# Routed experts of the second layer in shared blocks: column tiles of 64 and 32 slots on TensorE

## The chip, the cores and the metric

The kernel runs on one core of one Trainium2 chip. The metric is the device time of one execution in microseconds (us), taken as the median of several runs. A profiled execution gives the trace from which all rows below are read.

## What is computed

A transformer of two layers over 4 x 256 = 1024 tokens of width 256. Each layer is `x + attention(layernorm(x))` and then `x + ffn(layernorm(x))`. The change lies in the feed-forward part of the second layer, a mixture of 60 routed experts of which each token takes four, beside a shared expert:

```python
logits = x @ gate_w.T
probs = jax.nn.softmax(logits.astype(jnp.float32), axis=-1)
weights, sel = jax.lax.top_k(probs, TOP_K)            # TOP_K = 4 of E = 60
cw = jnp.zeros((M, E), jnp.float32).at[jnp.arange(M)[:, None], sel].add(weights)
def step(acc, ews):
    w13_e, w2_e, cw_e = ews                           # w13: 2 * 176 x 256, w2: 256 x 176
    gu_e = x @ w13_e.T
    h = jax.nn.silu(gu_e[:, :I]) * gu_e[:, I:]
    return (acc + cw_e[:, None] * (h @ w2_e.T), None)
sparse, _ = jax.lax.scan(step, jnp.zeros((M, H), jnp.float32), (w13, w2, cw.T))
return (shared + sparse).reshape(orig_shape)
```

1024 tokens with four experts each are 4096 pairs, on average 68 per expert. The counts per expert follow from the reference's routing of its inputs.

## The kernel before

Five instruction streams run side by side: PE (matmuls), ACT, DVE, POOL (which also issues the indirect DMAs) and SP (which issues the weight loads). They meet at semaphores. All matmuls of this part are float32; each of them shows as two records in the trace.

The second layer's feed-forward is two parts of one block of instructions.

`route_shared_l1` computes the router and the shared expert. DVE turns the routing into a table: a token's rank within its expert gives a slot of a block of 128 slots, block e for expert e, and slots past 128 of an expert go to further blocks behind the 60, which are handed out in expert order. Two tables result, `m.row` (the row of each slot) and `m.row_w` (its weight). They are built by matmuls of one-hot matrices (`table`, line 1846; DVE fills at lines 2003 and 2006, one tile of tokens after the other) that are interleaved by hand with the matmuls of the shared expert (lines 1812 and 1828). `further_blocks` (lines 1713 to 1723) then works out how many further blocks there are and which expert each serves; it ends with `over_ready`. POOL fetches the first eight blocks' rows in this part.

`routed_l1` works through the blocks. For block b:

- POOL gathers 128 rows of x from DRAM (`fetch`, line 1728), eight blocks ahead of the scatter (`FETCH`).
- PE turns them (`turn_x`, line 2099, two transposes, three blocks ahead); ACT copies (line 2161).
- PE multiplies with `w13` (`gate_up`, line 2111, two matmuls of 352 streamed columns, two blocks ahead). The stationary operand is the block's tokens (128 columns); the expert's weights stream.
- ACT takes the SiLU (line 2167), DVE multiplies (line 2193), PE turns the hidden rows (`turn_hid`, line 2120, one block ahead), ACT copies (line 2180).
- PE multiplies with `w2` (`outputs`, line 2132, two matmuls of 256 columns, 88 rows each).
- DVE scales by `row_w` into one of four buffers (line 2207), POOL scatters 128 rows to DRAM (`send`, line 2072).

So PE's order within a step is turn_x(b + 3), gate_up(b + 2), turn_hid(b + 1), outputs(b). Weights of 24 experts lie in SBUF as a ring (`RING`), loaded in pairs; twelve experts are loaded before the feed-forward part and twelve during it. SP reloads a pair's place when `outputs` of both its blocks has run (`y_ps`). For a further block SP reads the expert's number from memory (`load_further`, lines 1702 to 1710).

`all_rounds` sets the order: every engine waits for `over_ready` and loads the count of further blocks (line 2039) before its first block; it then runs 60 blocks, and behind nested tests of the count (line 2044) up to three rounds of twelve. Each round drains the order above and starts it anew. When all scatters have landed, `combine_and_store` reads each token's four rows, adds them and stores the result.

## Time and profile before

| | us |
|---|---|
| median of 3 runs | 832.78 (830.38 to 833.06) |
| span of the profiled execution, first to last instruction | 796.0 |
| median less span | 36.8 |
| routed stage, first gate_up matmul to last matmul | 582.5 to 764.7 |
| last scatter issued by POOL | 772.8 |
| combine and store | 776.9 to 796.0 |

| engine | busy us of the span |
|---|---|
| PE matmul | 677.6 (85%) |
| DVE | 439.8 (55%) |
| ACT | 322.9 (41%) |
| POOL | 298.2 (37%) |

A time for the profiled execution itself, other than its span, is not listed, so the 36.8 us stand for what lies around the span. The trace has 72 scatters: 60 blocks and one round of twelve. Matmul records overlap: a record is longer than the distance to the next start. Busy shares of PE are therefore read together with the distance between starts.

### The profile page before, as it was taken

How to read it: one execution, taken by the hardware profiler on the slowest of the kernel's cores; microseconds unless marked ns; L12 is line 12 of the kernel's file. 1: busy time of each engine (PE TensorE's matmuls, PEld its weight loads, DVE VectorE, ACT ScalarE, POOL GpSimd, SP SyncE). 2: the span in 40 equal slices, each digit the busy share in tenths (PEclk: the TensorE clock that was granted, in tenths of full speed). 3: DMA queues.
4: the chain of work that ended last, by engine and by line, in shares of the span. 5: the costliest groups of instructions: out<-in, count | busy, mean ns of one | idle time of the engine just before them, and what ended most of it. 6: DMA issues, size and time to landing. Idle time of an engine off the chain costs nothing. (4 is left out here: it accounts for less than half of the span.)

```text
span 796.0 us, 12037 instructions
## 1 busy us (share of the span) xinstructions
PE 677.6 (85%) x3794; PEld 441.6 (55%) x3794; DVE 439.8 (55%) x1182; ACT 322.9 (41%) x666; POOL 298.2 (37%) x449
## 2 busy tenths in 40 slices
PE   1667888895999999995699995999999999999940
PEld 1443444453766666763455563657677677777730
DVE  4658888854404569677776634589513333333315
ACT  1324777873232223421366673321243333333310
POOL 5440111101234233222013332122567777777760
PEclk9976999997699999997789997799999999999985
DMA  3185222001402555447343101950149999996347
GB/s 112 35 267 156 62 62 63 22 2 44 125 1 66 150 175 175 146 146 186 76 121 82 44 2 32 313 160 0 30 107 307 268 286 290 295 304 230 100 104 264
DMA packets 82904, 107.62 MB, mean 135 GB/s; under 512 B 10707, under 2 KB 57004, under 8 KB 82836
## 3 DMA queue, kind: packets, MB, share of 16 engines
q1 hardware_dynamic: 72820, 83.07, 35.3%
q0 software_dynamic: 7808, 20.05, 9.3%
q10 hardware_dynamic: 2208, 3.67, 1.2%
q8 instruction: 34, 0.56, 0.3%
q14 instruction: 34, 0.28, 0.1%
HBM read 82.47 MB, written 24.14 MB: 134 GB/s over the span
## 5 line engine op out<-in xcount | busy, mean ns | idle before, releaser
L769 DVE TENSOR_REDUCE l_mx<-ps 128x2 f32<-128x512 f32 (+2 forms) x256 | 125.7, 550 | 43.9 <-PE ps L629 43.6
L857 ACT ACTIVATE l_prob<-ps 128x1024 f32<-128x1024 f32 x96 | 98.5, 1027 | 25.5 <-PE ps L659 25.2
L629 PE MATMUL ps<-l_ks,l_qs 48*128 48x256 bf16 (+1 forms) x384 | 71.7, 300 | 26.0 <-DMA l_qs<-l_q_stacks 12.9
L1728 POOL DMA_INDIRECT xg<-x_rows,r_empty x80 | 78.9, 987 | 28.8 <-issue 19.8
L1392 DVE SCALAR_TENSOR_TENSOR xs<-ps,comb,xs 128x256 f32<-128x256 f32 x128 | 55.8, 481 | 59.3 <-PE ps L1052 59.2
L2072 POOL DMA_INDIRECT y_rows<-r_at_blk,row x72 | 71.5, 993 | 24.1 <-issue 17.4
L2193 DVE TENSOR_TENSOR r_hot<-r_hot,ps 128x176 f32<-128x176 f32 x72 | 24.3, 338 | 91.6 <-ACT r_hot L2167 91.6
L674 PE MATMUL ps<-l_prob,v 128*9 128x256 f32 (+1 forms) x768 | 69.9, 388 | 1.1 <-ACT l_prob L857 1.1
L1141 POOL TENSOR_TENSOR r_ehid<-r_erelu 128x512 f32<-128x512 f32 x32 | 35.6, 1112 | 83.5 <-ACT r_erelu L1245 83.5
L629 PEld LDWEIGHTS ps<-l_ks,l_qs 48*128 48x128 bf16 (+1 forms) x384 | 29.6, 102 | 57.6 <-issue 21.3
L1052 PE MATMUL ps<-f_w,r_ehid 128*128 128x256 f32 x256 | 60.8, 380 | 0.2
L2207 DVE TENSOR_SCALAR r_at_blk<-ps,row_w 128x256 f32<-128x256 f32 x72 | 34.8, 484 | 46.1 <-DMA y_rows<-r_at_blk,row 25.8
L1052 PEld LDWEIGHTS ps<-f_w,r_ehid 128*128 128x128 f32 x256 | 48.4, 190 | 21.1 <-issue 13.9
L1041 PE MATMUL ps<-xT,f_w 128*128 128x512 f32 x128 | 60.0, 592 | 0.0
L597 POOL TENSOR_TENSOR attn<-rest,l_rec 128x32 f32<-128x32 f32 x64 | 14.5, 247 | 113.7 <-DVE l_rec L788 113.7
L659 PE MATMUL ps<-l_qs,l_ks 50*128 50x256 bf16 (+1 forms) x384 | 56.5, 281 | 0.0
L2161 ACT COPY r_at_low<-ps 128x256 f32<-128x256 f32 x75 | 27.8, 372 | 55.6 <-PE ps L2099 55.6
L597 POOL TENSOR_TENSOR l_ctxv<-rest,l_rec 128x64 f32<-128x64 f32 x64 | 17.7, 298 | 82.7 <-DVE l_rec L788 82.7
L2111 PE MATMUL ps<-ew,r_at_low 128*128 128x352 f32 x144 | 48.5, 460 | 0.0
L2111 PE MATMUL ps<-ew13b,r_at_low 128*128 128x352 f32 x144 | 48.4, 459 | 0.0
L2167 ACT ACTIVATE r_hot<-ps 128x176 f32<-128x176 f32 x72 | 22.9, 318 | 59.0 <-PE ps L2111 59.0
L1812 PE MATMUL ps<-xT,r_sw 128*128 128x512 f32 x88 | 41.7, 614 | 0.0
(278 smaller groups left out, 1224.0 us busy)
## 6 DMA issues: line engine op xcount, KB each, us to landing
ew<-in_L_w SPq DMA_DIRECT2D x18, 704.0 KB
ew13b<-in_L_w SPq DMA_DIRECT2D x12, 704.0 KB
f_w<-in_L_w SPq DMA_DIRECT2D x32, 256.0 KB, 2.9
ew<-in_L_w SPq DMA_DIRECT2D x18, 352.0 KB
ew2b<-in_L_w SPq DMA_DIRECT2D x12, 352.0 KB
ew13b<-in_L_w SPq DMA_DIRECT2D x12, 352.0 KB
l_k_stacks<-part SPq DMA_DIRECT2D x8, 384.0 KB, 3.5
l_ks<-l_k_stacks SPq DMA_DIRECT2D x32, 96.0 KB, 2.3
```

The costliest lines, as they stand in the source:

```text
L629: ins = nc.tensor.matmul(ps[:, score_bank(n) + k, qt * S:(qt + 1) * S], qs[row:row + R, u % NBUF, col, qt * P:(qt + 1) * P], ks[row:row + ...
L659: ins = nc.tensor.matmul(ps[:, 2 + 2 * (n % 2) + k, kt * S:(kt + 1) * S], ks[row:row + lay.krows, b, col, kt * P:(kt + 1) * P], qs[row:row ...
L674: ins = nc.tensor.matmul(ps[row:row + W, 6, (c % 2) * S:(c % 2 + 1) * S], v[:, n // UP // GR * QT + kt, head, :], prob[:, n % PROBS, k, kt ...
L769: ins = nc.vector.reduce_max(mx[:, u % 2, :, s, head], one[:, :, lo:hi], AX_X)
L857: nc.scalar.activation(prob[:, n % PROBS, :, :, :].rearrange("p h k q -> p (h k q)"), ps[:, 2 + 2 * (n % 2):4 + 2 * (n % 2), :].rearrange( ...
L1041: ins = nc.tensor.matmul(m.ps[:, n % 2, :], m.f0_up[:, n % WSLOTS, c, :], m.xT[:, c, half * HT:(half + 1) * HT], start=(c == 0), stop=(c = ...
L1052: nc.tensor.matmul(m.ps[:, 2 + t, 0:D], ehid[:, n % 2, t * P:(t + 1) * P], m.f0_down[:, n % WSLOTS, :], start=True, stop=True).then_inc(e_ ...
L1392: v.scalar_tensor_tensor(m.xs[:, i, :], m.ps[:, 2 + t, 0:D], m.comb[:, i, e:e + 1], m.xs[:, i, :], ALU.mult, ALU.add).then_inc(e_added, 1)
L1728: nc.gpsimd.indirect_dma_start(m.xg[:, b % XBUF, :], None, m.x_rows, bass.IndirectOffsetOnAxis(m.token[:, b:b + 1], 0)).then_inc(m.x_loade ...
L1812: ins = nc.tensor.matmul(ps[:, 2 * (q % 2) + a, :], sw13[:, k, own], m.xT[:, k, h * TILES * P:(h + 1) * TILES * P], start=(k == 0), stop=( ...
L2072: nc.gpsimd.indirect_dma_start(m.y_rows, bass.IndirectOffsetOnAxis(m.row[:, b:b + 1], 0), yb[:, b % YBUF, :], None).then_inc(y_sent[b % YB ...
L2111: ins = nc.tensor.matmul(ps[:, b % 2, 0:2 * I1], xgT[:, b % 4, c * P:(c + 1) * P], w13[:, s, c, :], start=(c == 0), stop=(c == KD - 1))
```

## The change

Four experts share three blocks. Of each expert the first 64 tokens take half of block 3g or 3g + 1 of its group g; the next 32 take a quarter of block 3g + 2. Tokens past 96 go to units of 64 slots, two to a block, behind the 45 shared blocks. Which columns of a block belong to which expert is fixed in `tenants`; gate_up and outputs issue one matmul per tenant and half of the contraction, with the tenant's 64 or 32 tokens as the stationary operand and the tenant's weights streaming, into that tenant's partitions of PSUM. Eight unit blocks always run (`FIRST` = 45 + 8); the count is tested for more than 16, 32 and 48 units. The order of a step is kept, and it now runs through the rounds without draining: each engine runs to `FIRST - ahead`, then waits for `over_ready`, loads the count and tests it, and either goes on into the next round or runs its last `ahead` steps (SP 8, POOL 8, PE 3, ACT 3, DVE 2). PE's first transposes wait for `table_read` instead. A pair's place in the ring is reloaded after the third block of its group. POOL no longer fetches beyond the last block.

The routing on DVE changes with it: the counts are compared with 15 marks instead of 7, the slot of a token takes three cases instead of two, and tables have 77 columns instead of 96. One more small load, `starts`, brings the group offsets.

```diff
-ROUND = 12
-OVER = -(-(T * TOP1 // P) // ROUND) * ROUND
-BLOCKS = E1 + OVER
-FURTHER = OVER // ROUND
+HALF, FULL = 64, 96
+BASE = E1 // 4 * 3
+ROUND, FURTHER = 8, 3
+FIRST = BASE + ROUND
+BLOCKS = FIRST + FURTHER * ROUND
+OVER = 2 * (BLOCKS - BASE)
+MARKS = -(-(T - FULL) // HALF)
+SPARE = -(-BLOCKS // TOP1)
...
+def tenants(b):
+
+    if b >= BASE:
+        w = E1 + 2 * (b - BASE)
+        return ((0, HALF, w), (HALF, HALF, w + 1))
+    g, r = divmod(b, 3)
+    if r < 2:
+        return ((0, HALF, 4 * g + 2 * r), (HALF, HALF, 4 * g + 2 * r + 1))
+    return tuple((k * (FULL - HALF), FULL - HALF, 4 * g + k) for k in range(4))
+
+
+def pair_first(b):
+
+    return None if b < BASE and b % 3 == 2 else tenants(b)[0][2] // 2
+
+
+def pair_last(q):
+
+    return 3 * (q // 2) + 2 if 2 * q < E1 else BASE + q - E1 // 2
+
+
+def slot_starts():
+
+    e = np.arange(E1)
+    whole = 3 * P * (e // 4) + HALF * (e % 4)
+    rest = 3 * P * (e // 4) + 2 * P + (FULL - HALF) * (e % 4) - HALF - whole
+    return np.stack([whole, rest, BASE * P - FULL - whole - rest]).astype(np.float32)
...
-def further_blocks(nc, link, m, cmp, over_f, incl):
-
-    v, iota, half = nc.vector, m.iota, OVER // 2
-    for a in range(2):
-        own = slice(a * half, (a + 1) * half)
-        link(v.tensor_tensor(cmp, bcast(incl[:], 1, half), bcast(iota[:, own], 2, E1), ALU.is_le))
-        link(v.tensor_reduce(over_f[:, 1 + a * half:1 + (a + 1) * half], cmp, AX_X, ALU.add))
+def further_blocks(nc, link, m, flat, over_f, incl):
+
+    v, iota, own = nc.vector, m.iota, 2 * ROUND
+    cmp = flat[:, 0:own * E1].rearrange("p (o e) -> p o e", e=E1)
+    for a in range(0, OVER, own):
+        link(v.tensor_tensor(cmp, bcast(incl[:], 1, own), bcast(iota[:, a:a + own], 2, E1), ALU.is_le))
+        link(v.tensor_reduce(over_f[:, 1 + a:1 + a + own], cmp, AX_X, ALU.add))
     v.tensor_copy(over_f[:, 0:1], incl[:, E1 - 1:E1])
-    link(v.tensor_scalar(cmp[:, 0, 0:OVER], over_f[:, 1:1 + OVER], float(E1 - 1), None, ALU.min))
+    link(v.tensor_scalar(flat[:, 0:OVER], over_f[:, 1:1 + OVER], float(E1 - 1), None, ALU.min))
     v.tensor_copy(m.over[:, 0:1], over_f[0:1, 0:1])
-    v.tensor_copy(m.over[:, 1:1 + OVER], cmp[0:1, 0, 0:OVER]).then_inc(m.over_ready, 1)
+    v.tensor_copy(m.over[:, 1:1 + OVER], flat[0:1, 0:OVER]).then_inc(m.over_ready, 1)
...
+        sp.dma_start(starts[:], io["starts"].partition_broadcast(P)).then_inc(ld, 16)
...
-        link(v.tensor_tensor(many, bcast(count[:], 2, NT - 1), bcast(marks[:, 0:NT - 1], 1, E1), ALU.is_gt))
+        link(v.tensor_tensor(many, bcast(count[:], 2, MARKS), bcast(marks[:], 1, E1), ALU.is_gt))
...
-        link(v.tensor_tensor(extra[:], count[:], iota[:, 0:E1], ALU.subtract))
-        link(v.tensor_scalar(shift[:], extra[:], float(E1 - 1), float(P), ALU.add, ALU.mult))
+        link(v.scalar_tensor_tensor(shift[:], count[:], float(HALF), starts[:, 2, :], ALU.mult, ALU.add))
         rank = ps[:, 7, 0:NT * E1].rearrange("p (i e) -> p i e", i=NT)
-        link(v.tensor_scalar(prob[:], rank, float(P), None, ALU.is_ge))
-        link(v.tensor_tensor(slot_of, prob[:], bcast(shift[:], 1, NT), ALU.mult))
-        link(v.tensor_tensor(prob[:], slot_of, rank, ALU.add))
-        link(v.scalar_tensor_tensor(slot_of, bcast(iota[:, 0:E1], 1, NT), float(P), prob[:], ALU.mult, ALU.add))
+        v.scalar_tensor_tensor(prob[:], rank, float(HALF), bcast(starts[:, 1, :], 1, NT), ALU.is_ge, ALU.mult)
+        link(v.scalar_tensor_tensor(slot_of, rank, float(FULL), bcast(shift[:], 1, NT), ALU.is_ge, ALU.mult))
+        link(v.tensor_tensor(prob[:], prob[:], slot_of, ALU.add))
+        link(v.tensor_tensor(slot_of, rank, bcast(starts[:, 0, :], 1, NT), ALU.add))
+        link(v.tensor_tensor(slot_of, slot_of, prob[:], ALU.add))
...
-        v.tensor_copy(m.row_w[:], ps[:, 6, BLOCKS:2 * BLOCKS])
-        further_blocks(nc, link, m, over_cmp, over_f, incl)
+        v.tensor_copy(m.row_w[:], ps[:, 6, BLOCKS:2 * BLOCKS]).then_inc(m.table_read, 1)
+        further_blocks(nc, link, m, blk_flat, over_f, incl)
...
-    def all_rounds(eng, run, settled=lambda last: None):
-
+    def all_rounds(eng, ahead, step):
+
+        for b in range(FIRST - ahead):
+            step(b, FIRST)
         eng.wait_ge(m.over_ready, 1)
-        blocks = eng.value_load(m.over[0:1, 0:1], min_val=0, max_val=OVER)
-        run(0, E1)
+        units = eng.value_load(m.over[0:1, 0:1], min_val=0, max_val=OVER)
         def further(r):
-            if r < FURTHER:
-                with eng.If(blocks > r * ROUND):
-                    run(E1 + r * ROUND, E1 + (r + 1) * ROUND)
-                    further(r + 1)
-                    settled(E1 + (r + 1) * ROUND)
+            end = FIRST + r * ROUND
+            if r == FURTHER:
+                for b in range(end - ahead, end):
+                    step(b, end)
+                return
+            with eng.If(units > 2 * (r + 1) * ROUND):
+                for b in range(end - ahead, end + ROUND - ahead):
+                    step(b, end + ROUND)
+                further(r + 1)
+            with eng.Else():
+                for b in range(end - ahead, end):
+                    step(b, end)
         further(0)
-        settled(E1)
     @block.sync
     def _(sp):
-        def loads(first, last):
-            for b in range(max(first, RING), last, 2):
-                sp.wait_ge(y_ps, b - RING + 2)
-                if b < E1:
-                    load_weights(sp, m, io, b)
+        def load(b, end):
+            q = pair_first(b)
+            if q is not None and q >= RING // 2:
+                sp.wait_ge(y_ps, pair_last(q - RING // 2) + 1)
+                if 2 * q < E1:
+                    load_weights(sp, m, io, 2 * q)
                 else:
-                    load_further(sp, m, io, b)
-        all_rounds(sp, loads)
+                    load_further(sp, m, io, 2 * q)
+        all_rounds(sp, ROUND, load)
...
-        def run(first, last):
-            for b in range(first, last):
-                if b + FETCH < BLOCKS:
-                    fetch(b + FETCH)
-                send(b)
-
-        def settled(last):
-            for b in range(last, min(last + FETCH, BLOCKS)):
-                pool.wait_ge(x_loaded[b % XBUF], 16 * (b // XBUF + 1))
-            for b in range(last - YBUF, last):
-                pool.wait_ge(y_sent[b % YBUF], 16 * (b // YBUF + 1))
+        def step(b, end):
+            if b + FETCH < end:
+                fetch(b + FETCH)
+            send(b)
+            if b == end - 1:
+                for a in range(end - YBUF, end):
+                    pool.wait_ge(y_sent[a % YBUF], 16 * (a // YBUF + 1))
         pool.wait_ge(m.added, NT)
-        all_rounds(pool, run, settled)
+        all_rounds(pool, FETCH, step)
...
-            w13, _, s = ring_slot(m, b)
-            if b % 2 == 0:
-                pe.wait_ge(m.ew_loaded[b % RING // 2], ring_loads(b))
+            q = pair_first(b)
+            if q is not None:
+                pe.wait_ge(m.ew_loaded[q % (RING // 2)], ring_loads(q))
             pe.wait_ge(xt_done, b + 1)
             if b >= 2:
                 pe.wait_ge(hid_done, b - 1)
             for c in range(KD):
-                ins = nc.tensor.matmul(ps[:, b % 2, 0:2 * I1], xgT[:, b % 4, c * P:(c + 1) * P], w13[:, s, c, :],
-                                       start=(c == 0), stop=(c == KD - 1))
+                for row, n, w in tenants(b):
+                    w13, _, s = ring_slot(m, w)
+                    ins = nc.tensor.matmul(ps[row:row + n, b % 2, 0:2 * I1], xgT[:, b % 4, c * P + row:c * P + row + n],
+                                           w13[:, s, c, :], start=(c == 0), stop=(c == KD - 1))
             ins.then_inc(gu_ps, 1)
...
-            _, w2, s = ring_slot(m, b)
             pe.wait_ge(ht_done, b + 1)
             if b == 0:
                 pe.wait_ge(m.y_copied, NT)
             if b >= 2:
                 pe.wait_ge(y_done, b - 1)
             for c in range(2):
-                ins = nc.tensor.matmul(ps[:, 4 + b % 2, 0:D], hidT[:, b % 2, c * P:(c + 1) * P], w2[:, s, c, :],
-                                       start=(c == 0), stop=(c == 1))
+                for row, n, w in tenants(b):
+                    _, w2, s = ring_slot(m, w)
+                    ins = nc.tensor.matmul(ps[row:row + n, 4 + b % 2, 0:D], hidT[:, b % 2, c * P + row:c * P + row + n],
+                                           w2[:, s, c, :], start=(c == 0), stop=(c == 1))
             ins.then_inc(y_ps, 1)
-        def run(first, last):
-            if first == 0:
-                for b in range(3):
-                    turn_x(b)
-                m.last_outputs()
-                pe.wait_ge(m.shared_read, UNITS)
-            gate_up(first)
-            gate_up(first + 1)
-            turn_hid(first)
-            for b in range(first, last):
-                if b + 3 < BLOCKS:
-                    turn_x(b + 3)
-                if b + 2 < last:
-                    gate_up(b + 2)
-                if b + 1 < last:
-                    turn_hid(b + 1)
-                outputs(b)
-        all_rounds(pe, run)
+        def step(b, end):
+            if b + 3 < end:
+                turn_x(b + 3)
+            if b + 2 < end:
+                gate_up(b + 2)
+            if b + 1 < end:
+                turn_hid(b + 1)
+            outputs(b)
+
+        pe.wait_ge(m.table_read, 1)
+        for b in range(3):
+            turn_x(b)
+        m.last_outputs()
+        pe.wait_ge(m.shared_read, UNITS)
+        gate_up(0)
+        gate_up(1)
+        turn_hid(0)
+        all_rounds(pe, 3, step)
```

ACT and DVE are given the same form as PE: their work per block is as before, as `step(b, end)`, with 3 and 2 steps ahead. The number of blocks, 96 in the buffers before, is 77.

## Rows read from the trace of the kernel before

**Rows 1.** The first line of the page

```profile
span 796.0 us, 12037 instructions
```

**Rows 2.** Windows: us; busy PE, PEld, DVE, ACT, POOL; clock, DMA share, GB/s

```profile
680.00:720.00 40.00, 40.00 (x194) 29.59 (x193) 12.92 (x32) 15.53 (x49) 30.47 (x31) 1.00 0.99 302
```

**Rows 3.** Timeline, PE, one block: start, us, engine, line, shapes, count

```profile
659.87 1.35 PE L2111 MATMUL ps<-ew,r_at_low 128*128 128x352 f32 x4
...
661.05 0.38 PE L2120 MATMUL ps<-ident,r_hot 128*88 128x128 f32 x2
...
661.27 1.03 PE L2132 MATMUL ps<-ew,r_hot 88*128 88x256 f32 x4
...
662.36 1.35 PE L2111 MATMUL ps<-ew,r_at_low 128*128 128x352 f32 x4
```

**Rows 4.** The chain of waits, its end; start, us, what

```profile
756.07 0.97 POOL xg L1728
...
757.35 0.99 POOL y_rows L2072
...
772.79 3.17 DMA y_rows<-r_at_blk,row
...
776.88 4.64 DMA ew13b<-y_rows
```

**Rows 5.** Timeline, first and last matmuls of the stage, one scaling

```profile
582.46 2.63 PE L2111 MATMUL ps<-ew,r_at_low 128*128 128x352 f32 x8
...
762.06 0.48 DVE L2207 TENSOR_SCALAR r_at_blk<-ps,row_w 128x256 f32<-128x256 f32 x1 [0.40 <-PE ps L2132]
...
763.64 1.03 PE L2132 MATMUL ps<-ew2b,r_hot 88*128 88x256 f32 x4
```

**Rows 6.** Timeline, PE, attention of the first layer

```profile
100.31 0.39 PE L629 MATMUL ps<-l_ks,l_qs 48*128 48x256 bf16 x2
...
100.63 1.05 PE L674 MATMUL ps<-l_prob,v 128*9 128x256 f32 x16
...
101.61 0.44 PE L687 MATMUL ps<-ident,l_sumsT 128*128 128x128 f32 x2
```

**Rows 7.** Timeline, PE, attention of the second layer

```profile
431.22 1.06 PE L674 MATMUL ps<-l_prob,v 128*34 128x256 f32 x8
```

**Rows 8.** Windows, attention of the second layer

```profile
440.00:478.00 38.00, 36.48 (x275) 22.01 (x276) 19.38 (x65) 27.94 (x52) 12.84 (x46) 1.00 0.09 24
```

**Rows 9.** DMA over 591 to 733 by queue; one SP timeline row

```profile
DMA packets 16411, 40.40 MB, mean 284 GB/s; under 512 B 2546, under 2 KB 2546, under 8 KB 16396
...
q1 hardware_dynamic: 11178, 25.96, 59.8%
...
q0 software_dynamic: 5218, 14.27, 35.9%
...
590.32 25.73 SPq L1698 DMA_DIRECT2D ew<-in_L_w  x12
```

**Rows 10.** Lines 2044, 2039: instructions, ns min/median/max, first to last start

```profile
L2044 PEldq COMPARE_BRANCH  x2: 93/2386/4680, 733.3 to 763.5; - x2
...
L2044 ACTq COMPARE_BRANCH  x2: 44/47/50, 733.7 to 763.8; - x2
...
L2044 DVEq COMPARE_BRANCH  x2: 55/59/63, 734.6 to 766.8; - x2
...
L2039 PEldq TENSOR_LOAD <-over x1: 486/486/486, 575.1 to 575.1; - x1
...
L2039 PEldq FUSED_REGOPS  x1: 170/170/170, 575.6 to 575.6; - x1
```

**Rows 11.** DVE: two groups by line (busy, mean ns), one timeline row

```profile
L1979 DVE TENSOR_TENSOR r_at_blk<-r_count,r_marks 128x420 f32<-128x420 f32 x1 | 0.6, 596 | 0.0
...
L1718 DVE TENSOR_TENSOR r_at_blk<-r_incl,iota 128x1080 f32<-128x1080 f32 x2 | 2.6, 1278 | 0.0
...
584.30 0.34 DVE L2193 TENSOR_TENSOR r_hot<-r_hot,ps 128x176 f32<-128x176 f32 x1 [13.73 <-ACT r_hot L2167]
```

More of the change, by code:

```diff
@@ L1955, in _ @@
         v.memset(ones_e[:], 1.0)
-        v.tensor_scalar(marks[:], iota[:, 1:1 + NT], float(P), None, ALU.mult)
+        v.tensor_scalar(marks[:], iota[:, 0:MARKS], float(HALF), float(FULL), ALU.mult, ALU.add)
         dve.wait_ge(logit_ps, 1)
@@ L2363, in host_layout @@
     io["empty"] = np.arange(ROWS, ROWS + BLOCKS, dtype=np.float32)
+    io["starts"] = slot_starts()
     io["upper"] = np.triu(np.ones((P, P), np.float32), 1)
```

78 lines of the change are left out of this document (38 added, 40 removed).

## Prediction

> **What bounds the kernel now.** I read the windows by stage first. In the routed stage of the second layer PE is busy without a break at full granted clock, and the DMA engines are at 0.99 as well [rows 2]; so two resources are near their limit, and neither busy share names the bound. The timeline of one block gives PE's period: its gate_up matmuls start at 659.87 and those of the next block at 662.36, so 2.49 us, with no gap between any two groups [rows 3]. The chain of waits then shows that the end is not PE's: from 755 on (and from 725, rows alike) it runs through POOL alone, a gather and a scatter per block, 756.07 to 758.65, so 0.97 + 0.30 + 0.99 + 0.30 = 2.57 us with issue [rows 4]. PE's last matmuls run until 764.67 (763.64 + 1.03) [rows 5], while POOL sends its last rows at 772.79; their landing (3.17), 0.92 of settling and the combine from 776.88 close the span of 796.0 [rows 1, 4]. So the stage goes at POOL's pace, 2.57 per block, with PE 0.08 behind and DMA behind that.
>
> The time outside the span is 832.8 - 796.0 = 36.8 us; I have no other time for the profiled execution, so the sum is made on the span and the median added.
>
> **How many blocks.** The reference's routing of its inputs gives experts of 3 to 181 tokens. Eight exceed 128, hence one round of 12 further blocks: 72, as the trace has it (72 scalings and scatters). Past 96 there are exactly 16 units of 64 (14 experts are over 96; those of 178 and 181 take two, the other twelve, from 97 to 151, one). 16 fits the first 8 unit blocks, so 45 + 8 = 53 blocks run, and the test for more than 16 fails. No count lies on a threshold (the nearest below 97 is 88; below 160, 151), so rounding will not add a seventeenth.
>
> **Removed: 19 blocks.** POOL now does 45 times 2.57 plus 8 scatters alone at 1.29 (no fetch past the last block), 126 us, if never kept waiting. POOL stops being the bound; next late is PE, below.
>
> **Added: column tiles on PE.** Each gate_up and output matmul becomes two of 64 or four of 32 columns, each with its own weights streaming. If tiles of one set stream together, a set takes as long as one full matmul. The first layer's value matmuls have that form, f32 with 256 streamed columns in four column tiles: 16 records take 1.05 us [rows 6], where 4 full-width records of 256 columns take 1.03 [rows 3]. So four go at once. In the second layer, with two tiles of 34 columns, 8 records take 1.06 [rows 7]: two at once. I take the stream time of a block as unchanged.
>
> What is not free is the change between full and tiled array, four times per block (turn_x full, gate_up tiled, turn_hid full, outputs tiled). In full mode a group starts 0.17 or 0.16 before the recorded end of the one ahead (661.22 and 661.05; 661.43 and 661.27) [rows 3], since the records overlap. Into the tiles it is 0.07 (100.70 and 100.63), out of them 0.07 (101.68 and 101.61) [rows 6]: a gap of 0.10 each way. The first step in tiles is longer, by 0.03 with 34 columns (1.06 against 1.03); for 64 I take 0.05, bounds 0 and 0.10. The first transpose behind tiles is 0.06 longer (two take 0.44, in full mode 0.38); for the narrower turn_hid less, so 0.05. Per block: 4 x 0.10 + 2 x 0.05 + 2 x 0.05 = 0.60, so 3.09 us; bounds 2.9 and 3.2.
>
> The Trainium skill (TensorE: Matmul & The Clock Gate, Part 3, "The mechanism") says that a weight load overlaps a running matmul only when its row group differs, which column tiles of one block never do. The trace speaks against it: 16 records in the time of 4 leave no room for loads between them. By that rule the time would be that of the third rival.
>
> PE: 72 blocks took 764.67 - 582.46 = 182.2 us [rows 5], 2.9 over 72 x 2.49. Now 2.9 + 53 x 3.09 = 166.7, end 749.2.
>
> **The tail.** POOL no longer lags, so the scatter follows PE: 0.04 to DVE, 0.48 scaling [rows 5], 0.3 to POOL, 3.17 landing, 0.92 settling = 4.9: combine from 754.1 instead of 776.9, its 19.1 us unchanged. Span 773.2.
>
> **Moved: the count's test.** Loading the unit count and the If stood before the loop and between rounds; now every engine meets both shortly before its last steps. On PE: the load and the operation behind it 0.49 + 0.17, then the branch. Untaken it cost 0.09, taken 4.68, when PE had no work left after 764.67 [rows 5, 10]. Now the failed test jumps with three blocks still to finish. I take 0.7 + 4.68 less the 1.2 of matmuls under which the old branch began: +4.2, bounds 0 and 4.9. ACT's and DVE's branches show 0.05 and 0.06 [rows 10], but nothing that they do right after, so their price is 0 to 4.7 too: ACT's would lie beside PE's; DVE's comes after scaling block 50 with only 2.3 us of PE work left, so up to +3.7; I take 0, the row. SP's and POOL's meet slack (POOL needs 1.29 per block there against PE's 3.09, and has four y buffers).
>
> The Trainium skill (Runtime: NRT & Kernel Launch, "Instruction fetch mechanics") has a taken branch outside the fetched window wait for a fetch. If that holds for DVE as for PE, the upper bound of this term applies.
>
> **DMA.** Weights: 25.96 MB for 48 experts, 0.541 each [rows 9]; now 36 + 16 = 52, 28.1 MB, and 98 gathers and scatters of 0.131 MB, 12.8. At the 284 GB/s of 591 to 733 that is 144 us from about 593 (the first ring load was at 590.3 [rows 9] and now waits a block more, since three blocks free four experts): last weights at 737, 5.3 us of PE work behind them, 742.5. PE needs until 749: hidden by 7 us. Slower than 262 GB/s it would set the end.
>
> **Small edits.** The count comparison grows from 420 to 900 elements, twice (0.60 for 420, 1.28 for 1080: +0.5 each), one more 480-element operation (+0.7), one of 60 fewer (-0.2): DVE's first table is 1.5 us later and PE waits for it. Against that 64 table fills and 64 table matmuls shrink from 96 and 192 to 77 and 154 columns: 1.3 us on DVE (0.02 per fill, by the 1.0 ns per element of those two rows), 2.0 on PE (38 columns of 0.83 ns), spread over the stage. Net 0, bounds -2 and +1.5. further_blocks: 8 operations of 960 (1.15 each) for 4 of 1.28, +4 us in DVE's 13.7 idle [rows 11]; PE waits for the row weights now, not for it. One 0.7 KB load, at stage start: 0. SP's unit loads keep their form.
>
> Sum: 773.2 + 4.2 = 777.4 span, **814.2 us**, -2.2%.
>
> **Rivals.**
> - DMA floor: gaps cheaper, branch hidden; the end is 742.5 + 4.9 + 19.1 = 766.5, time 803; with 300 GB/s 801. For: the windows show 302 [rows 2]. Against: gaps seen in both attentions. 0.17.
> - Costlier finish: DVE's jump exposed, or DMA near 260 GB/s: 818 to 824. For: 4.68 on PE. 0.19.
> - Weight loads exposed in every step: eight steps per block at the 0.06 above, two counted already, +0.36 x 53 = 19: 829 to 833, no change. Against: [rows 6, 7]. 0.06. (The skill's rule on row groups, above, would act so.)
> - Slower: tiles stream one after the other. A 64-column block then costs one more 2.05 us of streaming (2.49 less four transposes of 0.11), a 32-column one three more: 38 x 2.05 + 15 x 6.15 = 170 us, time 984. It decides from a loss of 0.35 us per block (18.6 / 53), a sixth of the streaming. Against: [rows 6, 7]; for: those have 9 and 34 columns and the same 128 rows, outputs here use 88. 0.06.
> - Clock: gaps drop the grant to 1.2 GHz. The attention with the same gaps ran at 1.00, PE busy 36.5 of 38 [rows 8]; at half clock far slower, above 900. 0.03. A seventeenth unit, eight more blocks, +24: 838. 0.01.
>
> **How the numbers follow.** Forecast (809 to 817) 0.48. Range 801 to 825 holds 0.84: forecast, floor, costlier finish. A measurement tells about 0.3%, 2.5 us. Faster: 0.84 and half of the fourth case, 0.87; within 0.03; slower 0.10.
>
> **What would show it.** 544 gate_up records (38 x 8 + 15 x 16) in 53 blocks; block starts 3.0 to 3.2 apart with gaps of 0.10 at each change; POOL waiting for DVE; last PE work near 753, the combine from about 758; one branch on PE over 4 us shortly before its end. Wrong if the blocks' period is over 3.4, if PE waits for weights, or if the clock is below 1.00 in the loop.

## The result, and the profile after

| | before | after |
|---|---|---|
| median, us | 832.92 (830.38 to 835.52) | 779.86 (777.43 to 781.93) |
| ratio after/before | | 0.938, 95% interval 0.9348 to 0.9413 |
| span of the profiled execution | 796.0 | 776.8 |
| that execution's own time | not listed | 778.58 |

The change takes 53 us, not the 18.6 of the forecast, and the time lies below the whole range. Yet the forecast of the span was 777.4, and the span is 776.8. Both can be so only because the 36.8 us that I put outside the span do not lie there. One execution of the kernel before took 876.85 us at a granted clock of 0.80, and it is in no comparison below.

The changed kernel: the page's first line; the timeline of PE over two blocks (start, us, engine, line, shapes, count); the failed test and the last matmuls; the end of the chain of waits.

```profile
span 776.8 us, 12603 instructions
```

```profile
640.83 1.40 PE L2152 MATMUL ps<-ew,r_at_low 128*64 128x352 f32 x8
642.16 0.42 PE L2161 MATMUL ps<-ident,r_hot 128*88 128x128 f32 x2
642.51 1.07 PE L2174 MATMUL ps<-ew2b,r_hot 88*32 88x256 f32 x16
643.51 0.44 PE L2138 MATMUL ps<-ident,xg 128*128 128x128 f32 x2
643.88 1.39 PE L2152 MATMUL ps<-ew,r_at_low 128*32 128x352 f32 x16
645.20 0.42 PE L2161 MATMUL ps<-ident,r_hot 128*88 128x128 f32 x2
645.55 1.08 PE L2174 MATMUL ps<-ew,r_hot 88*64 88x256 f32 x8
646.57 0.44 PE L2138 MATMUL ps<-ident,xg 128*128 128x128 f32 x2
646.94 1.40 PE L2152 MATMUL ps<-ew,r_at_low 128*64 128x352 f32 x8
```

```profile
748.38 1.40 PE L2152 MATMUL ps<-ew,r_at_low 128*64 128x352 f32 x8 [2.02 <-issue]
...
751.42 1.95 PE L2174 MATMUL ps<-ew,r_hot 88*64 88x256 f32 x16
```

```profile
754.82 2.49 DMA y_rows<-r_at_blk,row
757.73 4.63 DMA ew13b<-y_rows
```

In this kernel gate_up is L2152, turn_hid L2161, outputs L2174, turn_x L2138. Eight records (two tiles of 64 columns) take 1.40 us and sixteen (four tiles of 32) take 1.39, where four at full width take 1.35 [rows 3]: the tiles of a set stream together. Blocks start at 640.83, 643.88 and 646.94, a period of 3.06. A group now starts 0.06 or 0.07 before the recorded end of the one ahead, where in full mode it is 0.16 or 0.17: the gap of 0.10 at each change that the attentions showed [rows 6]. The Trainium skill (TensorEngine Tiling (Array Packing), "Key Properties") says that a change of tiling mode drains TensorE; the trace agrees in so far as each change shows this gap.

### The profile page after: what moved, and what is told of

The parts are those of the page before. It is cut to its first block and busy times, and to the rows that moved or that the text cites. A ratio compares the mean times of both kernels' runs of the same rounds, so it can differ in the third digit from the quotient of the medians.

```text
span 776.8 us, 12603 instructions
## 1 busy us (share of the span) xinstructions
PE 658.9 (85%) x4224; PEld 377.0 (49%) x4224; DVE 427.4 (55%) x1148; ACT 304.9 (39%) x606; POOL 253.7 (33%) x403
## 5 line engine op out<-in xcount | busy, mean ns | idle before, releaser
L2115 POOL DMA_INDIRECT y_rows<-r_at_blk,row x53 | 52.3, 987 | 59.4 <-DVE r_at_blk L2245 51.9
L2234 DVE TENSOR_TENSOR r_hot<-r_hot,ps 128x176 f32<-128x176 f32 x53 | 17.9, 338 | 82.5 <-ACT r_hot L2209 43.9
L1761 POOL DMA_INDIRECT xg<-x_rows,r_empty x53 | 53.1, 1002 | 18.8 <-issue 14.5
L2245 DVE TENSOR_SCALAR r_at_blk<-ps,row_w 128x256 f32<-128x256 f32 x53 | 25.6, 483 | 51.5 <-remote 24.8
L2203 ACT COPY r_at_low<-ps 128x256 f32<-128x256 f32 x53 | 19.7, 373 | 59.4 <-PE ps L2138 33.9
L2152 PE MATMUL ps<-ew,r_at_low 128*64 128x352 f32 (+1 forms) x304 | 40.9, 468 | 2.3 <-issue 2.3
L674 PEld LDWEIGHTS ps<-l_prob,v 128*9 128x9 f32 (+1 forms) x768 | 26.8, 98 | 23.0 <-issue 10.2
L2209 ACT ACTIVATE r_hot<-ps 128x176 f32<-128x176 f32 x53 | 16.9, 320 | 51.9 <-PE ps L2152 25.5
```

The costliest lines, as they stand in the source:

```text
L674: ins = nc.tensor.matmul(ps[row:row + W, 6, (c % 2) * S:(c % 2 + 1) * S], v[:, n // UP // GR * QT + kt, head, :], prob[:, n % PROBS, k, kt ...
L1761: nc.gpsimd.indirect_dma_start(m.xg[:, b % XBUF, :], None, m.x_rows, bass.IndirectOffsetOnAxis(m.token[:, b:b + 1], 0)).then_inc(m.x_loade ...
L2115: nc.gpsimd.indirect_dma_start(m.y_rows, bass.IndirectOffsetOnAxis(m.row[:, b:b + 1], 0), yb[:, b % YBUF, :], None).then_inc(y_sent[b % YB ...
L2152: ins = nc.tensor.matmul(ps[row:row + n, b % 2, 0:2 * I1], xgT[:, b % 4, c * P + row:c * P + row + n], w13[:, s, c, :], start=(c == 0), st ...
```

## Experiments

Ratios are to the kernel before on the same chip, with 95% intervals. "Late starts" are a count of my own over a trace: for each of four hand-overs, the k-th group on PE against the k-th instruction that reads it on ACT or DVE, as L2099 to the copy L2161; late is a start over 0.3 us after both the recorded end of the group and the end of what ran before on the reader's engine. The recorded end of a matmul is the profile's model, but semaphore updates have times of their own in the trace.

### The kernel before, once more, and the changed one

> The kernel before, unchanged. Its profiled execution had a span of 796.0 us while its median is 832.9, and the changed kernel's executions take 1.8 us more than their spans (778.58 and 776.8). Theory A: the 36.8 us that I put outside the span lie inside it in the typical execution, so this run's span is near 831 and its trace shows where they go. Rival B: the time around the span really is 35 us for this kernel and 1.8 us for the changed one; then the span is near 796 and the time near 832.

Measured: 833.09 (827.09 to 835.86), ratio 0.9989 [0.9972, 1.0005]. The profiled execution took 827.09 with a span of 825.3: 1.8 us around the span, not 36.8, and 1.7 to 1.9 in every other execution, of all kernels here (776.8 and 778.58 of the changed one). So this profile is one of an ordinary execution, and the one that I read ahead of the prediction, 796.0, is not: with 1.8 it took 797.8, where the 75 others of the kernel before took 826.6 to 839. Where do the 29 us between the two lie? Windows of the ordinary one (us; busy PE, PEld, DVE, ACT, POOL; clock, DMA share, GB/s):

```profile
600.00:640.00 40.00, 35.01 (x161) 24.53 (x160) 10.02 (x25) 12.12 (x39) 26.39 (x27) 0.99 0.92 269
640.00:680.00 40.00, 38.30 (x166) 27.18 (x165) 10.90 (x27) 12.59 (x40) 25.85 (x28) 0.92 0.91 270
680.00:720.00 40.00, 33.09 (x147) 22.32 (x145) 10.03 (x25) 11.69 (x37) 25.37 (x26) 1.00 0.84 253
720.00:760.00 40.00, 34.68 (x155) 24.90 (x156) 10.50 (x26) 12.80 (x40) 25.54 (x26) 0.94 0.55 163
760.00:800.00 40.00, 35.63 (x154) 25.46 (x154) 11.23 (x27) 12.37 (x39) 26.01 (x27) 0.93 0.35 87
```

PE, 40.00 of 40 in the window of [rows 2], is idle for 2 to 7 of 40 us here, and the stage lasts from 580.27 to 796.37, 3.00 per block, in place of 182.2 us and 2.53 [rows 5]. DMA share and traffic fall towards the end; PE doesn't get faster. Over the stage PE is idle for 20.6 us, where the first profile has 1.7. Part of its work is also slower: the granted clock is at half (1.2 GHz) in four stretches of 17.1 us together, each behind idle times of PE, and never in the first profile's stage. Work of 17.1 us at half clock is worth half of that at full clock, so I estimate 9 of the 34 us between the two stages for the clock; the rest is idle time and what PE loses around it. What PE waits for shows in one block of the same trace, PE first, then ACT and DVE:

```profile
592.92 0.38 PE L2099 MATMUL ps<-ident,xg 128*128 128x128 f32 x2
593.14 1.35 PE L2111 MATMUL ps<-ew,r_at_low 128*128 128x352 f32 x4
...
597.19 0.42 PE L2120 MATMUL ps<-ident,r_hot 128*88 128x128 f32 x2 [0.21 <-DVE r_hot L2193]
```

```profile
595.01 0.37 ACT L2161 COPY r_at_low<-ps 128x256 f32<-128x256 f32 x1 [2.39 <-remote]
596.45 0.32 ACT L2167 ACTIVATE r_hot<-ps 128x176 f32<-128x176 f32 x1 [1.06 <-remote]
```

```profile
596.80 0.34 DVE L2193 TENSOR_TENSOR r_hot<-r_hot,ps 128x176 f32<-128x176 f32 x1 [2.71 <-issue]
```

turn_x ended at 593.30, its copy starts at 595.01. gate_up ended at 594.49, its SiLU starts at 596.45, though ACT was free from 595.38. In the trace of before, the same copy and SiLU start 0.04 us behind PE. The update of PE's semaphore has a time in the trace too: 594.99 for this turn_x and 596.42 for this gate_up, 0.02 or 0.03 us before the reader starts. In all 95 late starts of this trace the update stands less than 0.06 us before the start. So the reader is not slow: the signal of a finished matmul comes up to some microseconds late (PE's next groups, at 594.33 and 594.55, have long started by then), and the profile, which looks for a releaser close to the update, often writes "remote" or "issue". From 593 on this holds for 95 of 291 hand-overs behind PE, and never for ACT to DVE (SiLU to product). Before the stage the profile has next to no such wait (two of DVE and none of ACT before 560 in either profile of before, at most).

> The changed kernel, unchanged. Both theories: 778 to 782 us, span 1.8 us less. By theory A its ratio to the kernel before is 0.938 on this chip too.

Measured: 781.46 (780.06 to 785.4), ratio 0.9368 [0.9337, 0.9398]. The saving repeats. Both traces of the changed kernel have late starts too, so its profile was an ordinary one:

| late starts (us in sum) | gate_up to SiLU | turn_x to copy | outputs to scaling | turn_hid to copy |
|---|---|---|---|---|
| before, first profile (72 blocks) | 0 | 0 | 19 (17) | 0 |
| before, second profile (72) | 20 (21) | 28 (42) | 27 (45) | 20 (18) |
| after (53 blocks) | 10 (21) | 17 (22) | 21 (27) | 6 (5) |
| b_noring (72) | 25 (21) | 35 (55) | 33 (50) | 11 (9) |
| b_nogather (72) | 0 | 0 | 0 | 0 |
| b_spgather (72) | 0 | 0 | 0 | 0 |
| b_plainscatter (72) | 1 | 4 | 2 | 1 |
| b_poolbusy (72) | 0 | 2 (4) | 0 | 0 |
| b_twogathers (72) | 17 (23) | 32 (55) | 26 (46) | 12 (11) |
| b_padded (72) | 2 (2) | 2 (4) | 3 (6) | 1 |
| a_nogather (53) | 13 (5) | 0 | 0 | 1 (1) |
| a_full (53) | 14 (15) | 19 (28) | 17 (27) | 9 (11) |
| a_swap (53) | 13 (21) | 28 (25) | 24 (24) | 1 (1) |

The 19 of the first profile are of another kind. PE's signal is there on time in all of them, and the scaling waits until an earlier scatter out of its buffer has landed:

```profile
635.58 0.48 DVE L2207 TENSOR_SCALAR r_at_blk<-ps,row_w 128x256 f32<-128x256 f32 x1 [3.32 <-DMA y_rows<-r_at_blk,row]
```

What makes the signals late was tried with six edits of the kernel before.

### Weights

```diff
-            for b in range(max(first, RING), last, 2):
-                sp.wait_ge(y_ps, b - RING + 2)
-                ...
+            pass
...
```

> The kernel before, leaving out every weight reload of the ring (blocks from the 25th on compute with old weights). In the typical execution of the kernel before, ACT and DVE start 0.5 to 3 us after the PE matmuls that they wait for, in about a quarter of the handoffs; in the trace that the prediction was made from they never do. Theory L-DMA: these late handoffs come with the weight traffic. Then they are gone, POOL's 2.57 us per block is the bound, and the time is 796 to 800. Theory L-POOL: they come with POOL's indirect DMAs, which stay. Then 825 to 833.

Measured: 832.22 (829.06 to 833.04), ratio 0.9976 [0.9948, 1.0004], with as many late starts while the DMA engines ran at 0.27 to 0.29 of their time in place of 0.84 to 0.92. So the weight traffic is not the cause.

### Gathers

```diff
-                if b + FETCH < BLOCKS:
-                    fetch(b + FETCH)
                 send(b)
...
```

> The kernel before, leaving out the gathers of blocks 8 and later (PE turns the first eight blocks' rows again and again; the scaling multiplies by zero so that the scatters stay). Weight reloads and scatters stay. Theory L-POOL: half of POOL's work is gone, late handoffs become fewer or vanish, PE's 2.49 us per block is the bound, time 790 to 797. Theory L-DMA: weight traffic still makes them late, time 812 to 828.

Measured: 788.69 (787.7 to 790.03), ratio 0.945 [0.9425, 0.9476]. Without the gathers on POOL not one start is late, and 44 us are gone: POOL's pace explains 72 x 0.08 = 6 of them at most.

```diff
+        def plain(b):
+            ...
+            sp.dma_start(xg[:, b % XBUF, :], m.x_rows[r:r + P, :]).then_inc(x_plain[b % XBUF], 16)
...
```

> The kernel before with the 64 gathers of blocks 8 to 71 replaced by plain loads of 128 consecutive rows on SyncE's queue, the same bytes read into the same buffers (other rows, and the scaled rows multiplied by zero, so the output is wrong); GpSimd keeps the scatters. L-POOL: what makes TensorE's signals late is GpSimd's descriptor work for the gathers, so few late handoffs, a span like that without gathers: 787 to 793. L-TRAFFIC: it is the read traffic of the rows, so the late handoffs stay, 20 to 30 of 72 at each kind: 815 to 832.

Measured: 798.5 (796.61 to 805.66), ratio 0.9607 [0.9552, 0.9663]. The same bytes are read, the DMA engines are fuller than before, and no start is late:

```profile
600.00:640.00 40.00, 39.09 (x188) 28.28 (x187) 12.17 (x32) 14.75 (x47) 14.76 (x16) 1.00 1.01 296
640.00:680.00 40.00, 38.23 (x181) 27.00 (x180) 11.10 (x30) 14.21 (x45) 14.34 (x15) 1.00 1.01 296
```

PE's idle time here is waiting for its rows (5.7 us of turn_x before DMA xg<-x_rows in 600 to 740), which share a queue with the weights; that is the larger part of the 10 us over b_nogather. So the traffic of the rows alone does not make the signals late; the gathers have to be POOL's.

### Scatters

```diff
-            pool.wait_ge(y_done, b + 1)
-            nc.gpsimd.indirect_dma_start(m.y_rows, bass.IndirectOffsetOnAxis(m.row[:, b:b + 1], 0),
-                                         yb[:, b % YBUF, :], None).then_inc(y_sent[b % YBUF], 16)
+            pass
...
+            act.dma_start(m.y_rows[r:r + P, :], yb[:, b % YBUF, :]).then_inc(y_sent[b % YBUF], 16)
...
```

> The kernel before with its 72 scatters replaced by plain writes of 128 consecutive rows, issued from ScalarE's queue (rows land elsewhere, output wrong); GpSimd keeps the gathers alone, so it is busy half of the time. If gathers alone do it: the late handoffs stay at 20 to 35 of 72 and TensorE, no longer waiting for GpSimd, is still 0.3 to 0.5 us per block over its 2.49: 800 to 825. If it takes gathers and scatters together (GpSimd busy without a pause): few late handoffs, 785 to 795 plus what the 72 issues cost ScalarE.

Measured: 794.02 (792.84 to 795.07), ratio 0.9524 [0.9499, 0.955]. Eight late starts in all. The gathers alone do not do it either. Two fillings of the gap then tell a busy POOL from a POOL busy with indirect DMAs; both keep the scatters' release (`y_done`):

```diff
+            nc.gpsimd.indirect_dma_start(m.spare[:, b % 4, :], None, m.x_rows,
+                                         bass.IndirectOffsetOnAxis(m.token[:, b:b + 1], 0)
+                                         ).then_inc(m.spare_sent[b % 4], 16)
...
```

> The kernel before with each scatter replaced by a second gather of the same block into a spare buffer, released by the same signal (the scaled rows go out as plain writes on ScalarE's queue, other rows, output wrong): GpSimd issues indirect DMAs as before without a pause, but all of one kind. If it is GpSimd's issuing without a pause that makes TensorE's signals late: late handoffs at 20 or more of 72, 815 to 840. If it takes the scatters themselves (writes from SBUF to DRAM by the software queue beside gathers): few of them, 795 to 805.

```diff
+            nc.gpsimd.tensor_tensor(m.spare, m.spare, m.spare, ALU.add).then_inc(spare_set, 1)
...
```

> The kernel before with each scatter replaced by an addition of 128x512 on GpSimd (1.1 us, released by the same signal; the rows go out as plain writes on ScalarE's queue, output wrong): GpSimd as busy as before, with half of the indirect DMAs. If GpSimd's being busy is enough: late handoffs stay, 810 to 835. If it takes indirect DMAs one after the other: few, about the 794 of the kernel without the addition.

Measured: two gathers per block 831.99 (830.35 to 834.4), ratio 1.0028 [1.0009, 1.0048]; a gather and an addition 792.4 (791.56 to 794.87), ratio 0.9564 [0.9527, 0.96]. One window of each, two gathers first:

```profile
640.00:680.00 40.00, 35.91 (x161) 25.20 (x161) 10.02 (x25) 11.83 (x38) 25.89 (x28) 0.96 1.01 309
```

```profile
640.00:680.00 40.00, 40.00 (x194) 29.68 (x193) 13.13 (x32) 15.32 (x48) 32.26 (x33) 1.00 1.02 310
```

With the addition POOL is busier (32.26 of 40 us), the traffic is the same (310 GB/s), and PE has no gap. With a second gather in its place, PE loses 4.1 us of 40. So a busy POOL is not enough, and a gather does as well as a scatter: in these executions it takes two indirect DMAs a block from POOL, one after the other. The pair lies 39.6 us apart, of which 6 at most are POOL's pace (2.57 per block for PE's 2.49).

Two limits of this. First, every edit that takes an indirect DMA away takes its work away from POOL and from the software queue at once; no run tells POOL's issuing from that queue's work. Second, such issuing does not always do it: in the first profile POOL issued 107 indirect DMAs in a row, at most 0.31 us apart (636.34 to 773.78), and no signal of PE was late.

### Why it costs the changed kernel so little

```diff
-            for c in range(KD):
+            for c in (0, 1, 0, 1, 0, 0, 1):
                 ins = nc.tensor.transpose(ps[:, 6 + b % 2, c * P:(c + 1) * P], xg[:, b % XBUF, c * P:(c + 1) * P],
```

> The kernel before with five more transposes in each turn_x (the two of a block repeated into the same places: same result), 0.11 us each, so that TensorE's period without late starts is 2.49 + 0.55 = 3.04 us, about that of the changed kernel, for all 72 blocks. L-SLACK (GpSimd, which needs 2.57 of the period, then has time to catch up, and each hand-over behind TensorE has 0.55 us more before it is missed, so the late starts cost next to nothing): 72 x 3.04 = 219 us after 580, TensorE's end at 800, time 826 to 838, though 40 us of work are added. L-ADD (late starts cost their 0.5 us per block in any case): 860 to 875.

> The same without the gathers of block 8 and on (rows multiplied by zero, output wrong), its control: TensorE's period alone, 822 to 830 by both theories.

Measured: 835.58 (835.09 to 837.12), ratio 1.0069 [1.0047, 1.0092]; its control 829.71 (828.26 to 833.56), ratio 0.9988 [0.9964, 1.0011]. Five more transposes in each of 72 blocks, 40 us of work, cost the kernel before 5 us. PE with them (b_padded), then POOL:

```profile
700.55 1.03 PE L2132 MATMUL ps<-ew2b,r_hot 88*128 88x256 f32 x4
701.42 0.93 PE L2099 MATMUL ps<-ident,xg 128*128 128x128 f32 x7
702.19 1.35 PE L2111 MATMUL ps<-ew13b,r_at_low 128*128 128x352 f32 x4
703.37 0.38 PE L2120 MATMUL ps<-ident,r_hot 128*88 128x128 f32 x2
703.59 1.03 PE L2132 MATMUL ps<-ew2b,r_hot 88*128 88x256 f32 x4
```

```profile
702.39 0.99 POOL L2072 DMA_INDIRECT y_rows<-r_at_blk,row  x1 [0.77 <-DVE r_at_blk L2207]
703.68 0.97 POOL L1728 DMA_INDIRECT xg<-x_rows,r_empty  x1 [0.30 <-issue]
705.42 0.99 POOL L2072 DMA_INDIRECT y_rows<-r_at_blk,row  x1 [0.77 <-DVE r_at_blk L2207]
```

The period is 3.04, POOL waits 0.77 in each block, and only 8 starts are late in the whole trace. I had expected the late starts to stay and their cost to vanish in the slack; they mostly vanish themselves, once POOL pauses in every block. The eight fall between 758 and 773, where the further round begins and POOL issues up to eight indirect DMAs in a row; seven of them come at the fifth of a row or later.

In the changed kernel POOL's slack is as large, but it does not lie in every block. Of the trace of the changed kernel:

```profile
665.63 0.99 POOL L2115 DMA_INDIRECT y_rows<-r_at_blk,row  x1 [2.05 <-DVE r_at_blk L2245]
666.92 0.97 POOL L1761 DMA_INDIRECT xg<-x_rows,r_empty  x1 [0.30 <-issue]
668.19 0.99 POOL L2115 DMA_INDIRECT y_rows<-r_at_blk,row  x1 [0.30 <-issue]
...
675.14 0.99 POOL L2115 DMA_INDIRECT y_rows<-r_at_blk,row  x1 [2.11 <-DVE r_at_blk L2245]
```

A late signal makes POOL wait about 2 us; then it catches up with up to six DMAs in a row, and new late signals fall into that row. By the place of PE's end in POOL's row, 17 of 88 hand-overs are late at the first or second DMA, 25 of 55 at the third or fourth, 12 of 20 at the fifth or sixth, and none of 49 while POOL pauses. In b_padded it is 0 of 196 at the first or second. So rows of DMAs go with late signals within one trace as well; why the first and second differ between the two kernels stays open.

```diff
-            if b + FETCH < end:
-                fetch(b + FETCH)
             send(b)
...
```

> The changed kernel with only the first eight blocks' gathers (later blocks turn the same eight buffers again) and the scaled rows multiplied by zero; the scatters, the weights and every matmul stay, the output is wrong. Theory L-POOL (the late starts behind TensorE come with GpSimd's gathers, and cost the changed kernel little because its period of 3.06 us has slack that the old one had not): no late handoffs, TensorE's last outputs end at 749 to 752 us, time 773 to 778, that is 2 to 7 us under the changed kernel. Rival: the late starts cost per block what they cost before (35 us over 72 blocks, so 26 over 53): 755 to 760, or the weights' floor of 768 if that comes first.

Measured: 772.46 (768.64 to 775.27), ratio 0.9255 [0.921, 0.93] against 0.938 [0.9348, 0.9413] of the changed kernel: 7 us by the medians, 10 by the ratios. The 13 starts over 0.3 us that remain behind gate_up, all in blocks of four tiles, are 0.4 us each and cost nothing, since PE is busy for 40.00 of 40 us in each window between 600 and 720. That is about what the late starts still cost after the change, 0.14 to 0.2 us per block; the trace of the changed kernel has 6.5 us, in ten block periods over 3.06. Before they cost 0.5 per block (832.9 less 797.8, over 72).

### Mode changes, and what lies behind them

```diff
 def tenants(b):
+    return ((0, P, tenants_of(b)[0][2]),)
+
+def tenants_of(b):
...
```

> The changed kernel with one full-width matmul per block and half of the contraction in place of the column tiles (each block uses only its first expert's weights; loads, tables, gathers, scatters unchanged). No change of array mode. If the prediction's gaps (0.6 us per block) are the price and nothing else binds, the period goes from 3.06 to 2.49 and the time falls by 30 us to 750. If the weight traffic is a floor (the weights of 52 experts need until 740 or so), it falls by 5 to 14 us, to 767 to 775. Late PE handoffs, if they hit a shorter period harder, leave it near 775 to 780.

> The same without gathers, and each block's matmuls and loads at full width for its first tenant alone, so without mode changes between array shapes (output wrong; weights still stream as in the changed kernel). If nothing but TensorE's period of 2.49 us in place of 3.06 counted, 53 x 0.57 = 30 us would go: 745 to 750. If the weights bind (they landed at 741.6 us in the changed kernel, with five more us of work behind the last pair and 24 us of combine), TensorE waits at its weight semaphores and the time is 764 to 770: then the mode changes cost the changed kernel only the difference to that floor, about 10 us.

Measured: 771.19 (767.15 to 777.74), ratio 0.9219 [0.9173, 0.9266]; without gathers 751.32 (746.68 to 753.15), ratio 0.9011 [0.8966, 0.9056]. At full width the period is 2.49 again and 30 us of PE work are gone, but the time falls by 9 only, and without gathers by 21 (from 772.46). PE, idle for 21.4 us of a_full's stage, waits for weights in 6.3 of them:

```profile
729.70 2.33 PE L2157 MATMUL ps<-ew13b,r_at_low 128*128 128x352 f32 x4 [2.89 <-DMA ew2b<-in_L_w]
734.71 1.45 PE L2157 MATMUL ps<-ew13b,r_at_low 128*128 128x352 f32 x4 [0.56 <-DMA ew2b<-in_L_w]
739.10 1.45 PE L2157 MATMUL ps<-ew13b,r_at_low 128*128 128x352 f32 x4 [1.64 <-DMA ew2b<-in_L_w]
743.01 1.45 PE L2157 MATMUL ps<-ew,r_at_low 128*128 128x352 f32 x4 [1.15 <-DMA ew<-in_L_w]
```

and in a_full_nogather from 707 on:

```profile
707.63 2.33 PE L2156 MATMUL ps<-ew13b,r_at_low 128*128 128x352 f32 x4 [2.27 <-DMA ew2b<-in_L_w]
```

So a floor set by the weights is real: PE meets it in both runs (6.4 us of waits in the second), and not in the changed kernel, where it waits for no weights. In a_full late starts are at work beside it (59 of them, and 17.1 us at half clock), so 771.2 bounds the floor from above: it lies at least 9 us below the changed kernel. Of the 20 us between a_full and a_full_nogather I can't say how much is this floor and how much the late starts; that the floor moves with the gathers' bytes is not shown.

```diff
-            if b + 2 < end:
-                gate_up(b + 2)
             if b + 1 < end:
                 turn_hid(b + 1)
+            if b + 2 < end:
+                gate_up(b + 2)
             outputs(b)
```

> The changed kernel with one line moved on TensorE: turn_hid(b + 1) ahead of gate_up(b + 2), so that the two full-width steps of a block follow each other and so do the two column-tiled ones: two mode changes a block in place of four. If a mode change costs what the changed kernel's gaps say, 0.14 us each and more where loads no longer hide, the period falls by 0.2 to 0.3 us to about 2.8, 53 x 0.28 = 15 us at most: 765 to 770 us. Rival: turn_hid then comes sooner behind the step that DVE's product and ScalarE's copy answer, has less cover, and TensorE waits for them; or GpSimd, at 2.57 of 2.8 us with next to no pause, makes more signals late, as before: 775 to 785.

> The same without the count's load and test (the number of rounds fixed): a_swap less about 2 us.

Measured: 782.49 (781.01 to 790.5), ratio 0.9463 [0.9394, 0.9533]; without the test 777.29 (774.94 to 780.71), ratio 0.9378 [0.9331, 0.9426]. Two mode changes fewer in each block shorten the block less than I costed. Where nothing is late, the timeline of a_swap has:

```profile
642.65 1.39 PE L2152 MATMUL ps<-ew,r_at_low 128*32 128x352 f32 x16
643.97 1.08 PE L2174 MATMUL ps<-ew,r_hot 88*64 88x256 f32 x8
...
645.58 1.40 PE L2152 MATMUL ps<-ew,r_at_low 128*64 128x352 f32 x8
646.81 1.03 PE L2174 MATMUL ps<-ew,r_hot 88*64 88x256 f32 x8
647.77 0.44 PE L2138 MATMUL ps<-ident,xg 128*128 128x128 f32 x2
648.05 0.38 PE L2161 MATMUL ps<-ident,r_hot 128*88 128x128 f32 x2
648.36 1.40 PE L2152 MATMUL ps<-ew,r_at_low 128*64 128x352 f32 x8
```

The block that begins at 645.58 takes 2.78 us, its two tiled steps having the same width; where the widths differ, as at 642.65 (32 and 64 columns), the second starts 0.07 before the end of the first and not 0.17, and the block takes 2.93. Two in three of the 45 shared blocks are of that kind, so some 45 x 0.18 + 8 x 0.28 = 10 us of PE work are saved. None of it arrives: PE is busy for 34.39 to 37.45 of 40 us between 600 and 720, and POOL, with 2.57 of 2.78 us taken, makes 28 of 53 turn_x copies and 24 scalings start late (17 and 21 in the changed kernel). That fits the second of the rivals in its expectation.

### The test of the count

```diff
-        units = eng.value_load(m.over[0:1, 0:1], min_val=0, max_val=OVER)
-        ...
-        further(0)
...
+        for b in range(FIRST - ahead, FIRST):
+            step(b, FIRST)
```

> The changed kernel without the load of the unit count and without the tests on PE, ACT, DVE and POOL (and SP): 53 blocks straight through, same result. By the prediction's step the test costs 4.2 us on PE before block 52: 776 to 777. By the stall that the changed kernel's trace shows there (2.0 us): 778. If other engines' tests cost as well: 774 or less. If nothing: 780 to 781.

Measured: 779.28 (776.54 to 783.71), ratio 0.932 [0.9295, 0.9346]. Against a1_after's 0.9368 the test costs 4 us by the ratios and 2 by the medians, and by the medians of the pair of a_swap 5. The intervals overlap both times, so that it costs anything is not clear of noise. The trace shows 2.02 on PE (748.38, above). In the profile of a1_after the clock fell as well: it is at half from 750.8 to the end of the stage, behind late starts and the test's stall.

```profile
751.40 2.61 PE L2152 MATMUL ps<-ew,r_at_low 128*64 128x352 f32 x8 [2.15 <-issue]
753.95 0.66 PE L2161 MATMUL ps<-ident,r_hot 128*88 128x128 f32 x2
```

These groups took 1.40 and 0.42 in the changed kernel's first profile, and PE's work behind the stall 9.3 us (751.40 to 760.71) instead of 5.0. What a stop of PE costs there thus differs from one execution to the next.

## Why the prediction was wrong, point by point

- **The failed step: "The time outside the span is 832.8 - 796.0 = 36.8 us".** It is 1.8 us. The other 35 lie in the routed stage of every ordinary execution: signals of PE come late (95 of 291 hand-overs), PE idles for it and runs 17.1 us at half clock. The profiled execution lacked this. I carried them over unchanged, so the forecast holds 35 us that the change takes away for the most part: 777.4 + 1.8 = 779.2 would have been the time, against 779.86, though partly by luck (see PE's end, below). No rival spoke of this, and the range held nothing for it, though a difference of 4.4% without a place was the largest unknown in the sum. "So the stage goes at POOL's pace" was read rightly from [rows 4], and is true of that execution alone: ordinary ones go at 3.00 per block, with PE and POOL both waiting.
- **Blocks: right.** 53 scalings, no further round.
- **Tiles stream together, period 3.09: right**, 3.06 for either kind of block. The Trainium skill's rule on row groups (TensorE: Matmul & The Clock Gate, Part 3, "The mechanism"), the third rival, does not hold for column tiles here: 16 records in 1.39 us. Serial tiles fell too. The clock's rival did not come true: the stage of this profile ran at 1.00, and where a1_after's fell to half, it was for the last 9.9 us.
- **PE's end 753.4: right in sum** (751.42 + 1.95 = 753.37), **by luck.** The stage began at 584.11, 1.65 later than [rows 5]; the second profile of before begins at 580.27, so executions differ by that much, and the small edits' share in it stays open. Late starts, of which the sum had none, took 6.5. Against them stand 1.6 for the period (53 x 0.03), 2.2 for the test (2.0 for 4.2), and 4.3 in "2.9 over 72 x 2.49": the stage, 169.3 less 6.5 and 2.0, is 1.4 under 53 x 3.06, not 2.9 over. The 2.9 held 2.2 of draining at the round's edge (4.66 between two gate_ups there) and 2.3 of waits in three other blocks (3.22, 3.87 and 2.67), and the changed kernel drains no round.
- **Tail 4.9, combine 19.1: right**, 757.73 - 753.37 = 4.4 and 776.8 - 757.73 = 19.1.
- **"POOL stops being the bound", and what that is worth: right in kind, wrong in size.** In an ordinary execution not 0.08 per block hung on POOL's two indirect DMAs but 0.5. b_padded shows it best: with a pause of POOL in every block the late starts go, and that gives back about what 40 us of added PE work take.
- **DMA hidden: right**, PE of the changed kernel waits for no weights. By how much is less sure: the first rival's floor of 766.5 would mean 768.3 with 1.8 around it, and a_full took 771.2, late starts included. (737 + 5.3 in the prediction is 742.3, not 742.5.)
- **Where the 53 us come from** (estimates from the numbers above): late starts cost 35 before (832.9 less 797.8) and 7 to 10 after, so 25 to 28 less. The other 25 to 28 are between the undisturbed execution of before, 797.8, and the changed kernel less its late starts, 770 to 773; the forecast's 18.6 is less, since its stage for the changed kernel was some 6.5 too long and stood in for late starts that it did not know of.

Open: why one execution of before, of 77, had no late signals. It differs in one more thing. It has a semaphore update on record for each of its 72 SiLUs, and the second profile has 32 records for as many; but b_nogather has 39 and no late start, so missing records alone don't mean late signals. All executions here were recorded, so whether recording itself has a part in the late signals isn't known. Open too: by what path POOL's indirect DMAs hold up PE's signals and not ACT's, and why the changed kernel's rows of DMAs begin at all, where b_padded with nearly the same slack has its first late start at 758. Its PE issues twice to four times as many matmuls; whether that matters wasn't tried.

## What to carry to other kernels

Set the profiled execution's span against the median before anything else: a per cent or more between them is a stretch of work that this profile does not show, it belongs in the range whole, and it may well hang on the thing that is changed. An engine that issues indirect DMAs without a pause can be a cost for others beside its own: see in the trace whether it pauses in every period, and not only what its mean pace is. And where two bounds lie within a few us per stage, price the second at once: taking the mode changes away saved 30 us of PE time here, and 9 of device time.

## What the hardware showed that was not expected

- Semaphore signals of PE's matmuls came 0.3 to 3.2 us late in 95 of 291 hand-overs while POOL issued indirect DMAs of 128 rows in rows of up to eleven (0.97 and 0.99 us each, 0.30 apart). So it was with two gathers a block too (831.99), and with the DMA engines at 0.28 as at 1.01; hardly or not at all with a gather and an addition of 1.04 us (792.4), with gathers alone (794.02) and with scatters alone (788.69). Signals from ACT to DVE were not late.
- This can be absent: in one execution of 77, the one profiled first, 107 such DMAs in a row went without a late signal.
- The idle times that late signals make can lower the clock: four stretches at half of full speed, 17.1 us of the 216 of the stage, in the second profile of before, and none in the first.
- A change between full array and column tiles cost PE 0.10 us each way; with longer first steps and loads, 0.57 per block of four changes (3.06 for 2.49). Between tiles of 64 and 32 columns the gap was 0.10 as well (a_swap, at 643.97).
- A taken branch with matmuls ahead of it stopped PE for 2.02 us, where the one at the end of the kernel before took 4.68 [rows 10].
